# Second normalisation of batches 4 and 5 moved from self attention to cross attention's steps 1, 2, 6 and 7

## What is computed

```python
x = x + attn(layernorm(x), Wq, Wk, Wv, Wp)              # causal self attention, 16 heads, 4 key heads
x = x + xattn(layernorm(x), ctx, ...)                   # cross attention, 16 heads, 375 context rows
x = x + ffn(layernorm(x), gate, expert_bias, ...)       # 8 experts, top 2, and a shared expert
```

## Time and profile before

| | |
|---|---|
| median of 3 runs | 561.45 us (560.05 to 563.21) |
| the profiled execution | 559.17 us, of which the span is 557.3 us |
| TensorE busy | 526.8 us, 95% of the span |
| VectorE busy | 400.8 us, 72% |
| ScalarE busy | 302.4 us, 54% |
| GpSimd busy | 282.6 us, 51% |

### The profile page before, as it was taken

The page is one execution under the profiler, slowest core; times in us unless marked ns, Lnnn a source line. Parts: engine busy times, 40 slices in busy tenths (PEclk is TensorE's granted clock), DMA queues, the critical chain, the costliest instruction groups (busy, mean ns, idle before and its releaser), DMA issues. The chain is left out here.

```text
span 557.3 us, 9714 instructions
## 1 busy us (share of the span) xinstructions
PE 526.8 (95%) x3440; PEld 374.2 (67%) x3443; DVE 400.8 (72%) x909; ACT 302.4 (54%) x693; POOL 282.6 (51%) x360
## 2 busy tenths in 40 slices
PE   4989999999989999999999999999999999999995
PEld 4667776767767666576666776677678766885442
DVE  5675797797586698866877467894576667786863
ACT  3164735635655677655776356775466653621430
POOL 0579643464715776812666215693154552572660
PEclk9999999999999999999999999999999999999999
DMA  8976745766451630243693333244030019125928
GB/s 248 271 266 219 229 140 155 272 188 203 173 172 52 170 132 2 38 97 112 177 279 86 80 95 84 42 77 76 0 115 8 1 34 420 35 81 111 211 96 263
DMA packets 46242, 76.77 MB, mean 138 GB/s; under 512 B 20082, under 2 KB 30100, under 8 KB 45300
## 3 DMA queue, kind: packets, MB, share of 16 engines
q1 hardware_dynamic: 42948, 63.60, 37.0%
q0 software_dynamic: 2224, 10.73, 8.8%
q10 hardware_dynamic: 1024, 1.84, 1.0%
HBM read 57.36 MB, written 28.23 MB: 154 GB/s over the span
## 5 line engine op out<-in xcount | busy, mean ns | idle before, releaser
L2133 POOL TENSOR_TENSOR xprob<-xprob,erec 128x375 f32<-128x375 f32 x112 | 93.9, 843 | 129.1 <-DVE erec L1751 128.8
L1340 ACT ACTIVATE xprob<-s_ps,nmax 128x375 f32<-128x375 f32 x112 | 64.0, 572 | 55.2 <-DVE nmax L1746 53.1
L1746 DVE TENSOR_REDUCE nmax<-s_ps 128x1 f32<-128x375 f32 x112 | 59.3, 536 | 0.0
L2126 POOL TENSOR_TENSOR prob<-prob,rec 112x1792 f32<-112x1792 f32 x8 | 25.5, 3184 | 51.5 <-DVE rec L1654 51.3
L62 PE MATMUL s_ps<-kvt,qt_hl 128*128 128x376 f32 x112 | 48.1, 429 | 2.0 <-ACT xprob L1340 1.3
L1729 DVE SCALAR_TENSOR_TENSOR pt_hl<-f_ps,pt_hl 125x384 f16<-125x384 f32 (+1 forms) x62 | 38.0, 613 | 13.7 <-ACT pt_hl L1318 12.6
L62 PE MATMUL k_ps<-ow,ctx_hl 128*128 128x512 f16 (+1 forms) x104 | 39.6, 381 | 0.0
L64 PE MATMUL k_ps<-ow,ctx_hl 128*128 128x512 f16 (+1 forms) x104 | 39.4, 379 | 0.0
L63 PE MATMUL k_ps<-ow,ctx_hl 128*128 128x512 f16 (+1 forms) x104 | 39.4, 379 | 0.0
L63 PE MATMUL s_ps<-kvt,qt_hl 128*128 128x376 f32 x112 | 37.4, 334 | 0.0
L64 PE MATMUL s_ps<-kvt,qt_hl 128*128 128x376 f32 x112 | 37.4, 334 | 0.0
(11 more groups left out here) (380 smaller groups left out, 1494.4 us busy)
## 6 DMA issues: line engine op xcount, KB each, us to landing
w<-w_dram SPq DMA_DIRECT2D x6, 1024.0 KB, 10.0
raw_b<-in_raw SPq DMA_DIRECT2D x8, 640.0 KB, 5.2
raw_m<-in_raw SPq DMA_DIRECT2D x8, 576.0 KB, 4.7
raw_q<-in_raw SPq DMA_DIRECT2D x8, 512.0 KB, 6.9
ow_dram<-bw_sb SPq DMA_DIRECT2D x8, 512.0 KB, 5.5
ow_raw<-ow_dram SPq DMA_DIRECT2D x8, 512.0 KB, 3.3
qw_raw<-aw_dram SPq DMA_DIRECT2D x16, 256.0 KB, 3.1
w_dram<-in_w POOLq DMA_DIRECT2D x8, 512.0 KB, 5.7
```

Source lines behind the costliest of these rows:

```text
L1340: act.activation(xprob[z][:, 0:L], s_bank(n, k)[:, 0:L], ACT.Exp, bias=nmax[:, z:z + 1], accum_out=esum[:, z:z + 1]).then_inc(xexp_done, 1)
L1746: dve.tensor_reduce(nmax[:, z:z + 1], s_bank(n, k)[:, 0:L], X, ALU.max, negate=True).then_inc(xmax_done, 1)
L2126: pool.tensor_tensor(prob[q][:, :, :, :], prob[q][:, :, :, :], rec[q][:, :, :].unsqueeze(3).broadcast_to([T, PER, GROUPS, T]), ALU.mult).t ...
L2133: pool.tensor_tensor(xprob[z][:, 0:L], xprob[z][:, 0:L], erec[:, z:z + 1].broadcast_to([128, L]), ALU.mult).then_inc(xp_ready, 1)
```

## The change

Batches 4 and 5 leave round 3: there `turn_x2`, `x2_part_high`, `x2_part_low` and `layernorm` are not done any more. Their statistics are taken in step 1 (`late_part`, two BATCH_NORM_STATS2), those of batches 6 and 7 in step 2, with the aggregates of all four, and GpSimd's roots at the end of step 2 are for four batches. The order of the late normalisations is 6, 7, 4, 5: 6 and 7 in step 3 as before, 4 in step 6, 5 in step 7, both as `INSIDE` pieces `X4` and `X5` with `second_normal` in `early_part`. The third of them writes `r_xn` behind `lay_blank`, so it waits for `rows_laid` at 16*6. `turn_probs(4, 0)` waits for `x1_added` in place of `x2_low`.

```diff
-    INSIDE = {3: ("X6",), ROUTED + 3: ("T0",), ROUTED + 5: ("G1", "T2"), ROUTED + 6: ("G3",)}
+    SECOND = (6, 7, 4, 5)
+    INSIDE = {3: ("X6",), 6: ("X4",), 7: ("X5",), ROUTED + 3: ("T0",), ROUTED + 5: ("G1", "T2"), ROUTED + 6: ("G3",)}
...
                 if q == 0:
-                    wait(pe, x2_low, c)
+                    if c == B - 2:
+                        pe.wait_ge(x1_added, c)
+                    else:
+                        wait(pe, x2_low, c)
...
-                if i:
+                if i and more:
                     turn_x2(i, 0)
                     turn_x2(i, 1)
...
-                if i:
+                if i and more:
                     x2_part_high(i, 0)
                     x2_part_high(i, 1)
...
-            def second_stats(b):
-                dve.bn_stats(stats_all[:, b, :], x_sb[:, b, :]).then_inc(dve_chain, 1)
-                own.n += 1
-                if b == B - 1:
+            def second_stats(bs):
+                for b in bs:
+                    dve.bn_stats(stats_all[:, b, :], x_sb[:, b, :]).then_inc(dve_chain, 1)
+                    own.n += 1
+                if B - 1 in bs:
                     dve.wait_ge(dve_chain, own.base + own.n)
-                    aggregate(dve, stats_all, norm, slice(B - 2, B), aggregated)
+                    aggregate(dve, stats_all, norm, slice(HALF, B), aggregated)
 
             def second_normal(b):
-                if b == B - 2:
+                z = SECOND.index(b)
+                if z == 0:
                     dve.wait_ge(norm0_ready, 3)
                 else:
-                    dve.wait_ge(filled, use(AT[f"X{b - 1}"], f"X{b - 1}") + 1)
+                    dve.wait_ge(filled, use(AT[f"X{SECOND[z - 1]}"], f"X{SECOND[z - 1]}") + 1)
+                if z == 2:
+                    dve.wait_ge(rows_laid, 16 * 6)
                 dve.tensor_scalar(xn0[:, :], x_sb[:, b, :], norm[0][:, b, 0:1], norm[1][:, b:b + 1],
                                   ALU.subtract, ALU.mult).then_inc(xn0_ready, 1)
...
                 if n == 3:
                     second_normal(B - 2)
+                if n in (6, 7):
+                    second_normal(n - 2)
...
                 if n in (1, 2):
-                    second_stats(B - 3 + n)
+                    second_stats(range(HALF + 2 * (n - 1), HALF + 2 * n))
...
-                if i:
+                if i and more:
                     layernorm(2 * (i - 1), x2n, x2_ready)
...
-                if i:
+                if i and more:
                     x2_part_low(i, 0)
                     x2_part_low(i, 1)
...
-                        pool.wait_ge(aggregated, B + 2)
-                        norm_scales(pool, own, norm, slice(B - 2, B), rsqrt_steps_of_pool)
+                        pool.wait_ge(aggregated, B + HALF)
+                        norm_scales(pool, own, norm, slice(HALF, B), rsqrt_steps_of_pool)
```

More of the change, by code:

```diff
@@ L1011, in turn_tokens @@
                 n, name = AT[f"T{b}"], f"T{b}"
-                pe.wait_ge(xn0_ready, 2 + b + 1)
+                pe.wait_ge(xn0_ready, len(SECOND) + b + 1)
                 turn(x_take(n, name), xn0, filled)
@@ L1016, in turn_second @@
                 n, name = AT[f"X{b}"], f"X{b}"
-                pe.wait_ge(xn0_ready, b - B + 3)
+                pe.wait_ge(xn0_ready, SECOND.index(b) + 1)
                 turn(x_take(n, name), xn0, filled)
@@ L1813, in tokens_normal @@
                     dve.wait_ge(norm0_ready, 4)
-                    dve.wait_ge(rows_laid, 16 * 6)
+                    dve.wait_ge(filled, use(AT["X5"], "X5") + 1)
                 dve.tensor_scalar(xn0[:, :], x_sb[:, b, :], norm[0][:, b, 0:1], norm[1][:, b:b + 1],
                                   ALU.subtract, ALU.mult).then_inc(xn0_ready, 1)
-            def second_stats(b):
-                dve.bn_stats(stats_all[:, b, :], x_sb[:, b, :]).then_inc(dve_chain, 1)
-                own.n += 1
-                if b == B - 1:
+            def second_stats(bs):
[3 more added lines that the diff above has]
+                if B - 1 in bs:
                     dve.wait_ge(dve_chain, own.base + own.n)
-                    aggregate(dve, stats_all, norm, slice(B - 2, B), aggregated)
+                    aggregate(dve, stats_all, norm, slice(HALF, B), aggregated)
             def second_normal(b):
-                if b == B - 2:
+                z = SECOND.index(b)
+                if z == 0:
                     dve.wait_ge(norm0_ready, 3)
                 else:
-                    dve.wait_ge(filled, use(AT[f"X{b - 1}"], f"X{b - 1}") + 1)
+                    dve.wait_ge(filled, use(AT[f"X{SECOND[z - 1]}"], f"X{SECOND[z - 1]}") + 1)
+                if z == 2:
+                    dve.wait_ge(rows_laid, 16 * 6)
                 dve.tensor_scalar(xn0[:, :], x_sb[:, b, :], norm[0][:, b, 0:1], norm[1][:, b:b + 1],
@@ L2225, in _ @@
                     if n == 2 and k == TILES - 1:
-                        pool.wait_ge(aggregated, B + 2)
-                        norm_scales(pool, own, norm, slice(B - 2, B), rsqrt_steps_of_pool)
+                        pool.wait_ge(aggregated, B + HALF)
+                        norm_scales(pool, own, norm, slice(HALF, B), rsqrt_steps_of_pool)
                         pool.sem_inc(norm0_ready, 1)
                     if n == ROUTED + 2 and k == 1:
-                        pool.wait_ge(aggregated, B + 2 + HALF)
+                        pool.wait_ge(aggregated, B + HALF + HALF)
                         norm_scales(pool, own, norm, FIRST_HALF, rsqrt_steps_of_pool)
@@ L2249, in _ @@
                     shared_low(n - STEPS + 3)
-            pool.wait_ge(aggregated, B + 2 + B - 1)
+            pool.wait_ge(aggregated, B + HALF + B - 1)
             norm_scales(pool, own, norm, slice(HALF, B - 1), rsqrt_steps_of_pool)
```

## The result

The changed kernel takes **570.85 us** (median of 4, 567.68 to 571.83) against 560.75 us (559.67 to 563.21) for the kernel before: ratio 1.0165, 95% interval 1.013 to 1.020. It is slower by 1.6%, about 10 us. The profiled execution takes 571.12 us, its span is 569.3 us. (Of six later executions of the change one took 750.6 us at a mean granted clock of 0.656; it was disturbed and is left out of what follows.)

A forecast was written before the change was run, and what follows sets the result against it. TensorE, busy 95% of the span, was taken as the bound. Terms -2.1 + 1.4 + 0.9 + 7.5 + 1.5 = +9.2 us on a 561.45 us median gave 570.7 us, range 566 to 575 us.

The forecast's parts named there:

- Self attention, -2.1: Last half round: without the x2n wait and turn, scores follow the context's turn as in round 0, 2.1 us less.
- Statistics, +1.4: Steps 1 and 2: VectorE's added statistics and aggregates delay steps 2 (0.65 us) and 3 (0.75 us), 1.4 us more.
- The ports: Batch 6's normalisation is long because GpSimd works beside it; order should stay; turned round, the sum falls about 0.7 us.
- Turns, +0.9: Steps 6 and 7: eight turns come in for the eight taken out of self attention, 0.9 us more.
- The wait, +7.5: Step 6: batch 4's normalisation waits for six transfers, the last landing at 293.66, so TensorE waits 7.5 us.
- The lower end of that wait: Step 6: were the `done_dram` fill, at 291.1, the last to land, the wait would be 5.0 us.
- The clock, +1.5: Behind step 6's gap: TensorE's return from the lower clock costs 1.5 us, bounds 0 and 4.4 us.
- The sum: All terms together give +9.2 us; on the 561.45 us median of three runs that makes 570.7 us, 1.6% more.
- Without the wait, +0.2: Without the wait for the six transfers the sum would be +0.2 us.
- the change gives what it looks like: Rival: the statistics also hide in VectorE's idle time, leaving -1.2 us, 560.2 us; chance 0.04.

The follow-up runs named there:

- experiment 1: Changed kernel, with batches 4 and 5 normalised into a buffer of their own, `r_xl`; 559.63 us against 560.02 us for the kernel before, ratio 0.9992.
- experiment 5: Changed kernel, with an own buffer for batches 4 and 5 and their statistics taken in mid step 2; 559.22 us against 560.30 us, ratio 0.9970.
- experiment 4: Kernel before, with one more unused BATCH_NORM_STATS2 at the end of steps 1 and 2; 561.87 us against 560.02 us, ratio 1.0043.
- experiment 6: Changed kernel, with the `done_dram` fill issued last from a second zero block and not waited for in step 6; 562.91 us, ratio 1.0039.
- experiment 2: Changed kernel, with the three small tables on their own semaphore, so step 6 waits for the three fills alone; 568.68 us, ratio 1.0162.
- experiment 3: Changed kernel, with 33 unread matmuls on TensorE ahead of its wait for batch 4; 570.68 us, ratio 1.0187.

## Why the prediction was right

**Forecast 570.7 us, measured 570.85 us.** It held by its steps up to routing; the last 2 us of the profiled execution come from something that it didn't have.

- **Self attention, -2.1.** Measured -2.06 (2.41 us from the context's turn to the scores, as in round 0), -2.03 and -2.05 in experiments 1 and 5. A stretch of the same kernel without the piece was the right measure. The wait and turn that are seen to go (2.35 us) would have been 0.3 too much. The reason given for the 0.3 was not the right one: from the mask to the scores TensorE takes 1.16 us, against 1.17 before. What it waits for is the copy of the query weight, 0.21 us in front of that weight's turn.
- **Statistics, +1.4.** Measured +1.28 in the change (0.60, 0.43, 0.25), 1.12 when tried alone in experiment 4. The size was right for step 2 (0.65). For step 3 it was 0.68 against 0.75, and came in two pieces as said: what the fourth tile's slack let through, then the turn of batch 6.
- **The ports.** Batch 6's normalisation takes 2.79 us in the change (2.69 before) and is the only long one of the four; that of batch 4 takes 0.55, and in experiment 1 both new ones take 0.53. So here the order of VectorE and GpSimd didn't turn round, as was assumed, the 0.7 us that it might have given back didn't come, and step 7 cost nothing but its turn. In experiment 6, at another place, it did turn round: GpSimd 0.25 us later, and VectorE's 0.73 us became 1.71. By the Trainium skill (SBUF — State Buffer, section "SBUF: two separate sides") whichever of the two has the shared ports first keeps them for its whole instruction and the other is held up. The traces of the change and of experiment 6 agree: each time one of the two is drawn out and the other takes its usual time.
- **Turns, +0.9.** Experiment 1 measures 0.75 (0.35 and 0.40): 0.15 too much. The 0.89 us of the earlier trace rows ran with both turns back to back; here each overlaps its neighbours.
- **The wait, +7.5.** Measured 7.44 and 7.6 us. The chain of argument held: shared memory, SyncE's late last issue, the landing 6.2 us later, 0.6 us on to TensorE. The landing was read at 293.66 and came at 293.0, while TensorE arrived 0.4 us sooner, shifted by what self attention had saved. Experiments 1 and 6 show the cause by taking the awaited transfers away and by bringing them forward.
- **The lower end of that wait**, 5.0 us with the `done_dram` fill as the last to land, was no bound: with the fills awaited alone (experiment 2) the gap was 7.0. The 15.9 us of the earlier trace rows are the 48th update on a shared semaphore and most likely not the fill's own landing, which experiment 2 reads as 17.9 us.
- **The clock, +1.5.** Measured about 1.6 in the stretch: net +9.11 less experiment 3's +7.01 and less the 0.5 us by which its transfers landed sooner. Seen from the other side: from 293.71 to about 297 TensorE worked at half speed, and half of that is 1.7 us.
- **The sum.** +9.2 was said, +9.11 is measured at step 8. From there to the end the profiled execution loses 2.2 us more in the second stretch at 1.2 GHz, which no step had. The four executions with the higher mean clock take about 568.2 us, 8 us above the kernel before. The median was hit because the base was set 2.3 us above the profiled execution, on a median of three (561.45 us), while 46 later executions of the kernel before have medians of 560.0 and 560.3 us. The two errors, about 1 us of base and 1 to 2 us of missing stretch, have opposite signs; that they nearly cancel is luck.
- **Without the wait, +0.2.** Experiment 1: net +0.04, ratio 0.9992. The rival *the change gives what it looks like* (-1.2 us) is experiment 5: net -1.20 us at 302.

## What to carry to other kernels

Ahead of moving a piece of work, list what its buffers share memory with at the new place: a wait that was free in step 11 cost 9 us in step 6, with every engine idle, since it waited for a queue of fills to run dry. A buffer of its own, 2 KB in each partition, removes it. And when the engine with idle time on average takes on more, place the work in a gap of its timeline: the same statistics cost 1.3 us ahead of a step's first maximum and 0.1 us in the middle of the next step.

## What the runs showed of the hardware

- **A landing on a shared semaphore is only a count.** The view gives 15.6 to 15.9 us for the 1792 KB fill where it shares its semaphore with the small tables issued behind it, and 17.9 us where it doesn't (experiment 2), though the last updates come at the same times. A bound taken from such a row was 2 us off.
- **A fill waits for those ahead of it.** Behind a 2688 KB fill the 1792 KB fill landed 17.9 us after its issue; issued once the other fills had landed it took 7.6 us (experiment 6). SyncE's next issues are held up for 4 to 7 us each in the meantime.
- **VectorE and GpSimd hold each other up.** VectorE's scaling of `ow` takes 0.73 us or 1.71 us, depending on 0.25 us in GpSimd's order; TensorE lost 0.9 us by it (experiment 6).
- **A gap of TensorE costs more than its length.** In the gap of 7.44 us, with nothing running, the granted clock fell to the 1.2 GHz level and came back only after TensorE had worked at it for over 3 us (change) or over 5 us (experiment 2). Behind the gap of 1.35 us in experiment 6 it stayed at 1.00.
- **The clock also falls in full work.** In the routing it stood at 1.2 GHz for some 7 us in the profiles of four kernels (change, experiments 1, 3 and 6), with TensorE busy without a break just ahead of it (in the change from 488 us on, and the clock fell at 491.7), and 2.2 us were lost. What brings it on stays open: the same order of work ran there without it in the kernel before and in experiments 2 and 5.
